# Expert attention: all of the second head's weights turned by transposing transfers, and the expert sums moved to VectorE over contiguous elements

## The reference

```python
ss_g, sd_g = sigmoid(x @ Ws) * top3, sigmoid(x @ Wd) * top3      # 8 heads x 5 experts a token
q = einsum('bthed,bthe->bhtd', (x @ Wq) as (8, 5, 64), sd_g)     # sum over the 5 experts
k, v = the same with Wkv and ss_g
attn = softmax(q * 64**-0.5 @ k.T)                               # 1024 x 1024 a head
out = attn @ v                                                   # 64 a head
y = sum over heads and experts of (out @ Wo) where sd_g's mask is set
x = x + y
```

## Time and profile before

| | |
|---|---|
| median of 3 runs | 2760.68 us (2760.38 to 2760.92) |
| profiled execution, span | 2759.2 us |
| PE busy | 2441.3 (88%) |
| DVE busy | 2004.9 (73%) |
| POOL busy | 1862.8 (68%) |
| ACT busy | 1517.2 (55%) |
| first expert stage, first product to its end | 1368 to 1990 us from the start |
| L2591, 384 multiplies | 314.3 busy, mean 822 ns |
| L2600, 120 sums of v | 155.6 busy, mean 1297 ns |
| L1603, 128 low parts | 87.5 busy, mean 684 ns |

### The profile page before, as it was taken

One profiled execution on the slowest core, in us unless ns is written; L12 is line 12 of the kernel. 1 busy time (PEld: TensorE's weight loads), 2 busy tenths in 40 slices (PEclk: granted clock), 3 DMA queues, 4 the chain that ended last, 5 costly groups with the idle time before them and its releaser, 6 DMA issues. The chain is left out here.

```text
span 2759.2 us, 57518 instructions
## 1 busy us (share of the span) xinstructions
PE 2441.3 (88%) x21822; PEld 1594.3 (58%) x21822; DVE 2004.9 (73%) x3570; ACT 1517.2 (55%) x2197; POOL 1862.8 (68%) x1738
## 2 busy tenths in 40 slices
PE   6787786886999999999788999999798889999986
PEld 3554544643566666667545666665534456666655
DVE  7999445455777777777588888887386888888872
ACT  4222122332888888888525666666462256665564
POOL 1888100001999999999457899998510578999984
PEclk9999788988999999999899999999898999999998
DMA  1000000002889988899612333333201133333332
GB/s 44 1 1 1 0 23 13 1 23 66 140 154 159 160 149 161 158 152 157 135 20 55 62 62 62 62 62 70 60 13 60 20 55 62 63 62 62 62 70 58
DMA packets 632753, 193.27 MB, mean 70 GB/s; under 512 B 614920, under 2 KB 623624, under 8 KB 632480
## 3 DMA queue, kind: packets, MB, share of 16 engines
q1 hardware_dynamic: 632480, 189.60, 37.0%
HBM read 20.70 MB, written 1.05 MB: 8 GB/s over the span
## 5 line engine op out<-in xcount | busy, mean ns | idle before, releaser
L2307 PE MATMUL banks<-g_w,normed_t 128*128 128x320 f32 x1536 | 494.9, 449 | 28.6 <-DVE g_scratch L2591 28.4
L1778 DVE TENSOR_REDUCE at_negmax<-banks 128x1 f32<-128x1024 f32 x256 | 301.6, 1220 | 153.5 <-PE banks L1690 153.5
L2591 DVE TENSOR_TENSOR g_scratch<-banks,g_gate 128x640 f32<-128x640 f32 x384 | 314.3, 822 | 106.9 <-PE banks L2307 103.4
L1755 POOL TENSOR_TENSOR at_p_lo<-at_p,at_p_hi 128x640 bf16<-128x640 f32 x256 | 356.1, 1408 | 12.8 <-ACT at_p_hi L1743 11.4
L1597 DVE TENSOR_REDUCE g_negmax<-banks 128x1 f32<-128x1024 f32 x256 | 310.8, 1219 | 59.7 <-PE banks L1507 59.4
L2307 PEld LDWEIGHTS banks<-g_w,normed_t 128*128 128x128 f32 x1536 | 263.7, 190 | 121.4 <-DVE g_scratch L2591 48.1
L1561 ACT ACTIVATE g_p<-banks,g_negmax 128x1024 f32<-128x1024 f32 x256 | 285.9, 1117 | 72.1 <-DVE g_negmax L1597 64.3
L1584 POOL TENSOR_TENSOR g_p_lo<-g_p,g_p_hi 128x512 bf16<-128x512 f32 x256 | 301.1, 1197 | 30.2 <-POOL g_z L2514 19.4
L1736 ACT ACTIVATE at_p<-banks,at_negmax 128x1024 f32<-128x1024 f32 x256 | 285.7, 1116 | 6.4 <-DVE at_negmax L1778 6.4
L1574 ACT CAST g_r_hi<-banks 128x512 bf16<-128x512 f32 x128 | 75.0, 586 | 379.1 <-PE banks L1522 379.1
L1690 PE MATMUL banks<-at_k_t,at_q 64*128 64x512 f32 x1024 | 257.7, 622 | 17.9 <-POOL at_k_t L2039 9.1
(11 more groups left out here) (426 smaller groups left out, 6644.2 us busy)
## 6 DMA issues: line engine op xcount, KB each, us to landing
at_swapped<-at_crossed SPq DMA_DIRECT2D x128, 128.0 KB, 2.8
g_w<-in_ex_w SPq DMA_DIRECT2D x2, 2880.0 KB, 11.7
f_w<-in_W SPq DMA_DIRECT2D x2, 1024.0 KB, 5.6
at_rope<-in_rope SPq DMA_DIRECT2D x1, 2048.0 KB, 10.1
at_t_hi<-at_p_hi SPq DMA_TRANSPOSE x128, 3.6
at_t_lo<-at_p_lo SPq DMA_TRANSPOSE x128, 3.6
g_t_hi<-g_p_hi SPq DMA_TRANSPOSE x128, 3.1
g_t_lo<-g_p_lo SPq DMA_TRANSPOSE x128, 3.2
```

Of the source, the lines that this page charges most:

```text
L1755: self.nc.gpsimd.tensor_tensor(self.p_lo[:, j % self.RING, h, :], self.p[:, j % 2, h, 0:self.BY_DMA * P], self.p_hi[:, j % self.RING, h, : ...
L1778: self.nc.vector.tensor_reduce(self.negmax[:, j % 2, h:h + 1], self.core.banks[:, first:first + 2, :], AX.XY, ALU.max, negate=True).then_i ...
L2307: nc.tensor.matmul(out[:, 0:ED], core.xt[:, at:at + P], w[:, kind * H + tile // (T * BATCH) * 2 + h, :], start=True, stop=True).then_inc(p ...
L2591: v.tensor_tensor(qk_product[:, tile % 2, kind] if kind < 2 else v_product[:, tile % 2], core.banks[:, bank:bank + 2, 0:ED].rearrange("p h ...
```

## The change

1. HeadStream: head 1's weights are no longer turned by TensorE. The cast and the subtraction of head 1 cover all 1024 columns (512 for head 0 as before), and each transposing transfer turns 1536 columns, not 1024. The tiles u, u_hi, u_lo, ScalarE's copy of head 1 and VectorE's low part of it are gone.
2. The expert sums: the weights are laid out with the expert innermost, so a tile's products lie as (channel, expert); VectorE sums q and k by one reduction of 1280 elements a tile, at the end of its step, and v by one of 640. GpSimd sums nothing. The order of VectorE's work before the loop follows.

```diff
 HeadStream
+    KEPT = CHUNK // P
+    TURNED = 2 * T - KEPT
+    WIDTH = (CHUNK, SEQ)
+    START = (0, CHUNK)
...
-        self.nc.scalar.copy(self.p_hi[:, j % 2, h, :], self.p[:, j % 2, h, 0:CHUNK]).then_inc(self.hi_ready, 1)
+        self.nc.scalar.copy(self.part(self.p_hi, j, h), self.p[:, j % 2, h, 0:self.WIDTH[h]]).then_inc(self.hi_ready, 1)
...
-        self.nc.gpsimd.tensor_tensor(self.p_lo[:, j % 2, h, :], self.p[:, j % 2, h, 0:CHUNK], self.p_hi[:, j % 2, h, :],
+        self.nc.gpsimd.tensor_tensor(self.part(self.p_lo, j, h), self.p[:, j % 2, h, 0:self.WIDTH[h]], self.part(self.p_hi, j, h),
...
-        sp.dma_start(dst[:, j % 2], src[:, j % 2].rearrange("p h n -> p (h n)"), transpose=True).then_inc(self.turned[j % 2], 16)
+        sp.dma_start(dst[:, j % 2], src[:, j % 2], transpose=True).then_inc(self.turned[j % 2], 16)
...
-    def dve_lo(self, dve, j):
...
 expert_attention_stage, TensorE
-                hs.transpose(pe, j, 0)
+                hs.transpose(pe, j)
...
-                hs.transpose(pe, j, 1)
...
 ScalarE
-                hs.act_copy(act, j, 1)
...
 GpSimd
-                if j + LEAD - 1 < TOTAL:
-                    sum_tile(j + LEAD - 1)
...
 VectorE
-                                core.banks[:, bank:bank + 2, 0:ED].rearrange("p h (e c) -> p h e c", c=D),
-                                gate[...].unsqueeze(3).to_broadcast([P, 2, E, D]),
+                                core.banks[:, bank:bank + 2, 0:ED].rearrange("p h (c e) -> p h c e", e=E),
+                                gate[...].unsqueeze(2).to_broadcast([P, 2, D, E]),
...
+            def sum_tile(tile):
+                v.tensor_reduce(tok[:, :, t].rearrange("p k h c -> p k (h c)"),
+                                qk_product[:, tile % 2].rearrange("p k h c e -> p k (h c) e"), AX.X, ALU.add).then_inc(tok_ready, 1)
...
-            for n in range(4 * T):
-                if n % 2 == 0:
-                    apply_gates(n, n % 4)
-                if n % 4 == 3 and n // 4 in DVE_SUMS:
-                    sum_early(n // 4)
+            for tile in range(T):
+                apply_gates(4 * tile, 0)
+                if tile:
+                    sum_tile(tile - 1)
+                apply_gates(4 * tile + 2, 2)
+            sum_tile(T - 1)
...
+            for tile in range(T, LEAD):
+                n = 6 * T + 4 * (tile - T)
+                apply_gates(n, 4)
+                if tile > T:
+                    sum_tile(tile - 1)
+                else:
+                    hs.dve_split_values(dve, 0)
+                apply_gates(n + 2, 6)
+            sum_tile(LEAD - 1)
...
-                hs.dve_lo(dve, j)
                 beside(2)
                 if j:
                     hs.dve_normalise(dve, j - 1)
+                if j + LEAD < TOTAL:
+                    sum_tile(j + LEAD)
```

More of the change, by code:

```diff
@@ L2187, in expert_attention_stage @@
         z_t = sb("z_t", [P, 3, P])
-        hs = HeadStream(core, ctx, tag, home=lambda j, h: 6 if h and j >= TOTAL - T else 4, sums=5)
+        hs = HeadStream(core, ctx, tag, sums=5)
         STEPS = UNITS * T
@@ L2206, in expert_attention_stage @@
         early_bank = lambda n: core.ps[n % 4 if n < 4 * T else 4 + n % 4]
-        def wait_values(eng, tile):
-            early = min(tile + 1, T) // 2
-            if tile - early:
-                eng.wait_ge(v_ready, tile - early)
-            eng.wait_ge(v_early, early)
-        def sums_before(tile, on_dve):
-            own = sum(t < tile for t in DVE_SUMS)
-            return own if on_dve else tile - own
-        def wait_tok(eng, tile):
-            eng.wait_ge(tok_ready, sums_before(tile, False))
-            if sums_before(tile, True):
-                eng.wait_ge(tok_early, sums_before(tile, True))
         def first(j):
@@ L2489, in _ @@
             ins.then_inc(counts_clear, 1)
-            def sum_tile(tile):
-                unit, t = tile // T, tile % T
-                if t in (0, 4) and unit:
-                    pool.wait_ge(qk_full, unit * 4 - 2 + t // 2)
-                pool.wait_ge(product_ready, (last_of(tile, False) + 1) // 2)
-                part = qk_product[:, t % 2]
-                step(g.tensor_tensor(part[:, :, :, 0:2], part[:, :, :, 0:2], part[:, :, :, 2:4], ALU.add))
-                step(g.tensor_tensor(part[:, :, :, 0], part[:, :, :, 0], part[:, :, :, 1], ALU.add))
-                g.tensor_tensor(tok[:, :, t], part[:, :, :, 0], part[:, :, :, 4], ALU.add).then_inc(tok_ready, 1)
             def route(j):
@@ L2515, in route @@
                 pool.sem_inc(z_ready, 1)
-            def sum_values(tile):
-                pool.wait_ge(product_ready, (last_of(tile, True) + 1) // 2)
-                part = v_product[:, tile % 2]
-                step(g.tensor_tensor(part[:, :, 0:2], part[:, :, 0:2], part[:, :, 2:4], ALU.add))
-                step(g.tensor_tensor(part[:, :, 0], part[:, :, 0], part[:, :, 1], ALU.add))
-                g.tensor_tensor(hs.v[:, tile, :, 0:D], part[:, :, 0], part[:, :, 4], ALU.add).then_inc(v_early, 1)
-            for tile in range(T):
-                if tile not in DVE_SUMS:
-                    sum_tile(tile)
-            for tile in range(0, T, 2):
-                sum_values(tile)
-            for tile in range(T, LEAD - 1):
-                sum_tile(tile)
             for j in range(STEPS):
@@ L3302 @@
     half = wkv.shape[1] // 2
-    give("ex_w", _np.stack([_np.asarray(inputs["L1_ffn_Wq"]), wkv[:, :half], wkv[:, half:]]))
+    inner = lambda a: _np.asarray(a).reshape(P, 8, 5, 64).transpose(0, 1, 3, 2).reshape(P, -1)
+    give("ex_w", _np.stack([inner(a) for a in (inputs["L1_ffn_Wq"], wkv[:, :half], wkv[:, half:])]))
     give("ex_gate", _np.concatenate([_np.asarray(inputs["L1_ffn_Ws"]), _np.asarray(inputs["L1_ffn_Wd"])], axis=1))
```

127 lines of the change are left out of this document (55 added, 72 removed).

## The result

| | before | after |
|---|---|---|
| median of all runs, us | 2760.8 (4 runs, 2760.4 to 2768.0) | 2793.8 (4 runs, 2791.6 to 2797.1) |
| ratio to before, 95% interval | | 1.0115 (1.0101 to 1.013) |
| span of the profiled execution | 2759.2 | 2792.3 |
| first expert stage, first gate multiply to last residual add | 611.0 | 627.4 |
| second expert stage, the same | 612.6 | 626.5 |

The changed kernel is 33 us slower; 21 were predicted. The two stages account for 16.4 + 13.9 = 30.3 of it. The span grew by 33.1; the rest (2.7 of it before the first gate multiply) lies in code that the change does not touch, and that code takes between 1533 and 1543 us in the eleven profiled executions of this study. One of the ten runs of `start_on_pool` (experiment 6) was slow throughout, 3802.5 us at a mean granted clock of 0.584, and takes no part in any comparison.

The account below looks back on a forecast made before the run. Plain steps were held by the two spare banks and VectorE's gate multiply, VectorE becoming late. Start 3.4, choosing 5.5, six units 0.5, end 1.3: 10.7 a stage, 21.4 for two, added to the 2760.7 median: 2782 us, range 2764 to 2805.

Parts of the forecast that it names:

- The plain step: Loop step with nothing special in it: VectorE becomes late by 0.13, 8.21 us, 0.04 more than before.
- Turning steps: Two steps a unit with eight transposes of q and k on TensorE: 9.05 us before, 8.95 with late scores.
- The transposes at 0.07: Head 1's four transposes on TensorE, 0.43 by themselves: the two-bank hand-over lets a plain step gain only 0.07 us.
- Rival 1: TensorE is the bound after all: the transposes give 0.43 in some 50 steps a stage, 2737 us; 5%.
- Rival 2: VectorE's new reduction runs at the strided rate, 2.6 instead of 1.49 us: 2928 us; 5%.
- The transfers: Transposing transfers of 1536 columns land in 4.0 us, between 3.2 and 4.8, hidden but with no cover left.
- Rival 3: Transfers land late, 4.8 instead of 4.0: +0.4 in some 38 steps a stage, 2812 us; 10%.
- The start: Start of the stage, first eight tiles, values and three tiles ahead: VectorE's multiplies and sums cost +3.4 us a stage.
- The choosing steps: Five steps, j 0 to 4, where VectorE waits almost nowhere: +1.15 us each, taken as +5.5 a stage.
- The split of v: One step a unit: the split waits for ScalarE's copy, now behind a later exp, some +0.35 us.
- The end: Last 8 steps, without projections: only the last transfer is waited for, +1.3 us a stage.
- Rival 4: Smaller losses, size not given in the text; 15%, of which a good half within the bound of no change.

Follow-up runs that it names:

- start_on_pool: `exchanged` with GpSimd's sums given back for the tiles it summed before, up to step 4 of the loop: 2768.3 us, ratio 1.0024.
- experiment 6: Two kernels: `start_on_pool` (2768.3 us), and the same with the low part of v of units 1 to 7 moved to GpSimd and two buffers of v (2753.8 us).
- exchanged: Changed kernel with its two sums exchanged: q and k between the multiplies of b1 and b2, v behind the normalisation: 2782.4 us, ratio 1.0078.
- experiment 3: Half of each gate multiply of the loop left out, in the kernel before (2752.5 us) and in `exchanged` (2743.9 us).
- transfers_only: Kernel before with the new HeadStream alone, GpSimd keeping its sums: 2843.6 us, ratio 1.0296.
- sums_only: Changed kernel with the old HeadStream, so head 1's transposes stay on TensorE: 2796.4 us, ratio 1.0128.
- experiment 5: Changed kernel with three product buffers for v, not two: 2789.2 us, with 2761.6 for the kernel before beside it.
- experiment 1: Each half of the change alone: `transfers_only` (2843.6 us) and `sums_only` (2796.4 us).

## Why the prediction was right in direction and short in size

- *The plain step* was right. VectorE became the late engine behind the multiply of b2; the chain worked out as 3.69 measured 3.67, and the plain step 8.18 against 8.21. `exchanged` confirms the cause by removing it. Turning steps came to 9.13, not to 8.95 (9.05 before): there the scores wait up to 0.38 for the copies of turned k on ScalarE, more than the 0.2 that I gave the later copies.
- *The transposes at 0.07* was right (0.06), and experiment 3 shows the reason. Rival 1 (faster) is ruled out as long as the multiply of 0.82 stands between two pairs; in u1 of `transfers_only` the plain step fell by 0.06 and no further.
- *The reduction* was right: 1.476. Rival 2 (strided rate) is ruled out. *The transfers* land in 3.8 to 4.0 and in units 1 to 6 TensorE waits for them less than before (1.0 instead of 3.7). Rival 3 is ruled out.
- *The start* was the term that was sized too small: +6.8 and +7.0 a stage where +3.4 stood. The prediction did not reckon with TensorE's granted clock, which reads 0.50 for 10.2 us of the start. With the clock at 1.00, in the first stage of `sums_only`, the same start takes 53.9, +3.2; with it at 0.91 it takes 57.5. That the +3.4 is met so closely at a clock of 1.00 is in part luck, for two errors stand against each other in it. The sum put VectorE's instructions back to back, 0.74 each, 11.8 for the values; they took 13.0, since every multiply waits for the sum before it on its own engine (experiment 5: 1.1). And the start of the kernel before, from whose rows it was reckoned, has 3.4 us at 0.50 itself. The three tiles ahead took 12.4 up to the maximum, where the prediction's rows give 11.2 (now 8.5); with the clock at 1.00 they take 11.0. The first eight tiles, reckoned at +0.1, took 1.1 more up to the first value; with the clock at 1.00 they take 30.1, 0.8 less than before.
- *The choosing steps*: +6.2 in the first stage and +3.9 in the second, against +5.5. Step 1 lost 2.1 in the first stage, with 3.4 us at a clock of 0.50, and 0.9 in the second, at 1.00, where 1.15 was reckoned; the later steps have 6.8 us more at 0.50 in the first stage and 3.4 in the second. So the +6.2 is near the forecast by luck: at the clock of the kernel before the term was 1.6 too large. My sum held the choosing's own instructions at what they took before, and they got shorter: 12.7 a stage instead of 14.0 (the 192-element add 0.73, from 1.12). In size that is most of the 1.6.
- *The split of v*: predicted +0.35 a unit for a late copy. In units 1 and 2 the split takes 1.24 instead of 1.99 and 2.00, and its step 8.89 instead of 9.06. In units 3 to 6 it takes 2.15 and the step 9.79, where the kernel before had 8.52 to 9.22. The late copy is there, 0.23 between the multiply of b1 and the split. But VectorE is the late engine in this step, and so the sum of q and k is paid here too: from the multiply of b2 to that of b0 3.66 instead of 2.26. At the 1.24 that it takes in `sums_only` the split would be 0.9 shorter; in the kernel before it was nearly as long (1.99 to 2.07 in units 4 to 6). The prediction did not price what GpSimd's longer subtraction does to the instruction beside it, which the rows of experiment 1 show.
- *The end*: +2.3 and +1.8 against +1.3. In the first stage the wait for the last transfer grew by 2.0, the whole of the longer subtraction and landing: the prediction had counted on the routing beside it to hide a part. With the old transfers (`sums_only`) the end is 85.3 as before.
- *Rival 4*, smaller losses, did not come. The choosing's instructions got shorter, but the sum of the deviations went to the larger side, with the clock in the start. The 3 us outside the two stages were in no term.

Together the terms were 10.7 a stage and came out at 16.4 and 13.9. In size the stretches at 0.50 match the difference: 3.6 in each start, and in unit 0 of the first stage some 2 more, by which it is longer than that of the second. The other deviations nearly cancel. What makes the clock fall where it does was not varied by itself.

## What to carry to other kernels

Take from an engine only what it is late by. Before an instruction's removal is counted, work out which hand-over (here two banks and a multiply) holds the step at the place where it stands; four transposes of 0.43 were worth 0.06. When work moves from a helping engine to one that is nearly full, price the start and the irregular steps by themselves: the plain step cost nothing here, and 13.0 of the 16.4 lay before the end of unit 0. And place a moved instruction in the gap that the profile shows: the same sums, some 3 us further up in the step, cost 11 us less (5.2 in the second stage, where the clock falls alike).

## What the runs showed of the hardware

- Two instructions of VectorE with two inputs from SBUF were longer behind a GpSimd instruction of that kind that was still under way: the comparison by 1.76 at 1.90 of overlap (0.95 to 2.71, `start_on_pool`), the low part of v by 0.91 at 1.06 (1.24 to 2.15, the changed kernel). In the pair where VectorE started first (1437.10 in the kernel before) it took 0.96, and GpSimd's add was the longer one (1.92 instead of 1.27). The reduction with one input took 0.95 in both, and the gate multiply, which reads a bank, took 0.80 to 0.84 in all its 384 cases in the kernel before.
- In the changed kernel TensorE's granted clock read 0.50 from 1406.6 to 1413.4, just behind a wait of 2.16, and from 1430.5 to 1433.9, behind waits of 0.84 and 1.03. The same waits in the first stage of `sums_only` came with 1.00 throughout, and the window 1436 to 1444 of the changed kernel, 5.22 busy of 8, reads 1.00 as well, so what sets the clock was not shown. In and around the stretch at 0.50 in choosing step 1 a pair took 1.73 instead of 1.34 and eight transposes 1.68 instead of 1.04, and the same start took 57.5 at a mean of 0.91 and 53.9 at 1.00.
- In the values of the start, where each multiply of VectorE waits for its own sum just before it, it is 0.91 from sum to multiply, and 0.73 with three buffers, without that wait: 0.17 to 0.18 for the wait, with nothing else late.
- Transposing transfers of 1024, 1280 and 1536 columns landed in 3.1 to 3.2 (kernel before), 3.6 (the attention stage, both kernels) and 3.8 to 4.0 (the changed kernel). There GpSimd's subtraction took 1.16 for 512 and 2.13 for 1024.
- The reduction over groups of 5 contiguous elements took 0.81 for 640 and 1.476 for 1280 in the changed kernel; with a step of 64 between the elements, in the kernel before, 640 took 1.29.
